# A decoder layer with routed experts: a first token set of seven tiles, routing spread over the attention's steps, marks on GpSimd, later norms on ScalarE

## What is computed

```
x = LN(x + attn(x))        h = LN(x)*gamma + beta; K = h Wk + bk; V = h Wv + bv
                           w = exp((K Wka + bka)/16);  w = w / cumsum(w)
                           attn = cumsum(w * K) * V
x = LN(x + xattn(x, ctx))  softmax(Q K^T / 4, masked) V Wo, 16 heads
logits = x router_w^T + router_b;  top 2 of 8 experts, softmax over the two
x = LN(x + sum over the 2 chosen experts of weight * (gelu(x w1^T + b1) w2^T + b2)) * ln_w + ln_b
```

## Time and profile before

| | us |
|---|---|
| median of 3 runs (542.98 to 546.97) | 543.5 |
| the profiled execution | 543.59 |
| its span on the core | 541.9 |
| TensorE busy | 496.7 (92%) |
| VectorE, ScalarE, GpSimd busy | 374.2, 250.0, 259.8 |

### The profile page before, as it was taken

The page is one execution under the profiler, slowest core; times in us unless marked ns, Lnnn a source line. Parts: engine busy times, 40 slices in busy tenths (PEclk is TensorE's granted clock), DMA queues, the critical chain, the costliest instruction groups (busy, mean ns, idle before and its releaser), DMA issues.

```text
span 541.9 us, 10883 instructions
## 1 busy us (share of the span) xinstructions
PE 496.7 (92%) x3283; PEld 446.7 (82%) x3283; DVE 374.2 (69%) x1111; ACT 250.0 (46%) x835; POOL 259.8 (48%) x370
## 2 busy tenths in 40 slices
PE   6778999989999869988999999999999999999960
PEld 6666888878888757887799999999999999999950
DVE  3777978868768977528877656766676666766644
ACT  3445676656766436652343444433434444333410
POOL 4444132222212320436467656766667666676553
PEclk9999999999999979999999999999999999999995
DMA  8009920836565543426466556666666565666210
GB/s 232 10 7 338 339 86 16 301 110 208 175 222 165 166 132 130 160 58 236 131 205 212 194 197 198 213 222 205 215 209 205 191 221 224 235 221 221 62 49 15
DMA packets 57568, 93.95 MB, mean 173 GB/s; under 512 B 12050, under 2 KB 49305, under 8 KB 52391
## 3 DMA queue, kind: packets, MB, share of 16 engines
q1 hardware_dynamic: 50263, 80.17, 44.2%
q0 software_dynamic: 5616, 12.82, 7.7%
q10 hardware_dynamic: 1632, 0.27, 0.3%
HBM read 65.64 MB, written 30.44 MB: 177 GB/s over the span
## 4 chain that ended last, share of the span: by engine, by line
PE 80%; DVE 11%; issue 3%; POOL 3%; ACT 2%; POOLq 0%; DMA 0%; DVEq 0%; SPq 0%; ACTq 0%
PE psum_a L1690 13%; PE psum_b L1690 12%; PE psum_v L1702 12%; PE psum_c L1702 11%; PE psum_b L1446 8%; PE psum_v L1579 6%; PE psum_a L1545 5%; PE psum_m L1597 2%; PE psum_m L1446 2%; PE psum_c L1566 2%; PE psum_m L1677 1%; PE psum_a L1548 1%; PE psum_c L1561 1%; PE psum_b L1453 1%; DVE front_then_w_ring L1050 1%
## 5 line engine op out<-in xcount | busy, mean ns | idle before, releaser
L954 ACT ACTIVATE front_then_w_ring<-psum_a,front_then_w_ring 128x128 f32<-128x128 f32 x160 | 45.7, 368 | 72.6 <-PE psum_a L1690 71.3
L864 ACT ACTIVATE work<-psum_a,score_max 128x77 f32<-128x77 f32 x256 | 62.2, 334 | 36.2 <-DVE score_max L1121 36.1
L1690 PEld LDWEIGHTS psum_a<-front_then_w_ring 128*128 128x128 f32 x640 | 74.5, 192 | 3.9 <-issue 3.0
L1690 PE MATMUL psum_a<-front_then_w_ring 128*128 128x128 f32 x640 | 75.1, 275 | 2.6 <-ACT front_then_w_ring L944 2.0
L954 ACT ACTIVATE front_then_w_ring<-psum_b,front_then_w_ring 128x128 f32<-128x128 f32 x152 | 43.2, 368 | 69.2 <-PE psum_b L1690 64.5
L1702 PE MATMUL psum_v<-expert_w,front_then_w_ring 128*128 x320 | 72.6, 380 | 0.1
L1690 PEld LDWEIGHTS psum_b<-front_then_w_ring 128*128 128x128 f32 x608 | 70.9, 192 | 0.9
L1690 PE MATMUL psum_b<-front_then_w_ring 128*128 128x128 f32 x608 | 71.1, 275 | 0.0
L1702 PE MATMUL psum_c<-expert_w,front_then_w_ring 128*128 x304 | 68.8, 379 | 0.0
L1702 PEld LDWEIGHTS psum_v<-expert_w,front_then_w_ring 128*128 128x128 f32 x320 | 59.3, 190 | 7.6 <-issue 0.4
L1702 PEld LDWEIGHTS psum_c<-expert_w,front_then_w_ring 128*128 128x128 f32 x304 | 56.3, 190 | 6.9
(11 more groups left out here) (232 smaller groups left out, 891.6 us busy)
## 6 DMA issues: line engine op xcount, KB each, us to landing
front_then_w_ring<-in_w1b SPq DMA_DIRECT2D x39, 1028.0 KB
weighed_outputs<-routing SPq DMA_DIRECT2D x16, 1024.0 KB, 6.7
expert_w<-in_w SPq DMA_DIRECT2D x8, 1024.0 KB, 10.5
weighed_outputs<-work SPq DMA_DIRECT2D x39, 128.0 KB
token_rows<-front_then_w_ring SPq DMA_DIRECT2D x16, 128.0 KB, 2.4
second_buffers<-in_x SPq DMA_DIRECT2D x4, 256.0 KB, 4.6
token_rows<-routing SPq DMA_DIRECT2D x1, 1024.0 KB, 5.3
front_weights_then_tail<-in_b SPq DMA_DIRECT2D x1, 1024.0 KB
```

Source lines behind the costliest of these rows:

```text
L864: last = act.activation(prob[:, u % RING_U, at_k:at_k + SC], pa[:, H % 2, g * SC:(g + 1) * SC], ACT.Exp, bias=smax[:, j % 2, head:head + 1])
L954: last = act.activation(hidT[t % 2][:, c, :], src[:, n, q * P:(q + 1) * P], ACT.Gelu, bias=bias[:, c:c + 1])
L1690: last = pe.matmul(dst[:, n, q * P:(q + 1) * P], w1[:, k, c * P:(c + 1) * P], xtT[t % 2][:, k, :], start=(k == 0), stop=(k == KD - 1))
```

## The change

1. FIRST is 7 instead of 8 and SETS is ((0, 7), (7, 9)): set 0 has 7 tiles and 14 pairs, set 1 has 9 tiles and 18 pairs. 32 more tiles wait for both sets. RANKS_STEP is 50.
2. VectorE's routing of set 0 stands in more steps: three operations at 41 (`first_top`), three at 44 (`first_hot`), the second choice at 47; counts, ranks, and the map's first half at 50, `map_of` and `place_later` at 51, `place` at 52. Marks at 53 to 56.
3. Of each mark pair, GpSimd makes the position one (`mark_slots`), VectorE the column one, with a semaphore of its own.
4. x1's norm from piece 3 on and x2's norm of tiles 0 to 13 are ScalarE's: GpSimd also makes the mean's negative and its product with the root.
5. The first expert tile uses psum_b. Tiles 0 and 1 are turned in steps 61 and 63 (psum_b too), and the passage is written in another order.
6. Second-set marks of GpSimd come in three runs: six pairs behind the row entries, six behind the later map's casts, six behind tile 1's gather (the program's rows below show it). ScalarE's `attention_step` calls `x1_normalise` for pieces from 3 on and `x2_normalise((H - 10) // QUADS)` in the steps that VectorE had. The store column of a tile is no longer limited and the second map column is gone (MAPS 3 to 2).

```diff
-FIRST = 8
+FIRST = 7
...
-SETS = ((0, TILES // 2), (TILES // 2, TILES // 2))
+SETS = ((0, FIRST), (FIRST, TILES - FIRST))
...
-RANKS_STEP = (CHUNKS - 1) * STEPS + 1
+RANKS_STEP = (CHUNKS - 1) * STEPS + 2
...
+                if t >= TILES - 2:
+                    pool.tensor_tensor(x2_rstd[:, j:j + 1], x2_veps[:, j:j + 1], mhalf[:, 0:1], ALU.pow).then_inc(x2_rstd_ready, 1)
+                    return
+                pool.tensor_scalar(x2_drop[:, j:j + 1], x2_mv[:, j, 0:1], -1.0, None, ALU.mult).then_inc(x2_drop_made, 1)
+                pool.tensor_tensor(x2_rstd[:, j:j + 1], x2_veps[:, j:j + 1], mhalf[:, 0:1], ALU.pow).then_inc(x2_pow, 1)
+                pool.wait_ge(x2_drop_made, t + 1)
+                pool.wait_ge(x2_pow, t + 1)
+                pool.tensor_tensor(x2_shift[:, j:j + 1], x2_drop[:, j:j + 1], x2_rstd[:, j:j + 1], ALU.mult).then_inc(x2_rstd_ready, 1)
...
+            def mark_slots(n, first_pair, end):
+                t0, nt = SETS[n]
+                pool.wait_ge(placed, 3 * n + 3)
...
+                for i in range(first_pair, end):
+                    c, t = divmod(i, nt)
+                    pool.tensor_scalar(at_pos[n][:, i], cols, part_n[:, c, t0 + t:t0 + t + 1], None, ALU.is_equal).then_inc(pos_ready, 1)
...
-                if H == RANKS_STEP - 1:
+                if H == RANKS_STEP - 2:
                     weigh(0)
-                if H == RANKS_STEP + 1:
+                if H == RANKS_STEP + 2:
                     map_tiles(0)
                     rows_of_choice(0)
...
+                    mark_slots(0, 0, 4)
+                if H == RANKS_STEP + 4:
+                    mark_slots(0, 4, 9)
+                if H == RANKS_STEP + 5:
+                    mark_slots(0, 9, SET_PAIRS[0])
...
-                if quad == 2 and H >= 10:
-                    x2_normalise((H - 10) // QUADS)
-                if piece_at("x1", H) is not None:
+                if piece_at("x1", H) is not None and piece_at("x1", H) < BY_ACT:
                     x1_normalise(piece_at("x1", H))
...
-                if H == (CHUNKS - 1) * STEPS - 3:
-                    first_choice(0)
-                if H == (CHUNKS - 1) * STEPS - 2:
+                if H == RANKS_STEP - 9:
+                    first_top(0)
+                if H == RANKS_STEP - 6:
+                    first_hot(0)
+                if H == RANKS_STEP - 3:
                     second_choice(0)
                 if H == RANKS_STEP:
                     first_map()
+                if H == RANKS_STEP + 1:
+                    map_of(tbend, spare, FIRST, 0.0)
+                    place_later()
+                if H == RANKS_STEP + 2:
                     place(0)
...
-                where, which = marks_of(n, i)
...
-                dve.tensor_scalar(where, cols, part_n[:, c, t:t + 1], None, ALU.is_equal)
-                dve.tensor_scalar(which, cols, part_n[:, TOPK + c, t:t + 1], token1[:, t:t + 1], ALU.is_equal,
-                                  ALU.mult).then_inc(pos_ready, 1)
+                dve.tensor_scalar(at_col[n][:, i], cols, part_n[:, TOPK + c, t:t + 1], token1[:, t:t + 1], ALU.is_equal,
+                                  ALU.mult).then_inc(col_ready, 1)
...
-            route_logits(TILES - 1)
-            first_choice(LAST)
-            second_choice(LAST)
             indices(2)
             weigh_output(0)
             add_input(0)
+            route_logits(TILES - 1)
+            first_top(LAST)
+            first_hot(LAST)
+            second_choice(LAST)
...
-            for i in range(SET_PAIRS[LAST] // 2):
-                mark(LAST, i)
             dve.wait_ge(ln_in, 2 * 16)
-            indices(3)
             weigh_output(1)
             add_input(1)
             sum_row(0)
-            for i in range(SET_PAIRS[LAST] // 2, SET_PAIRS[LAST]):
+            for i in range(SET_PAIRS[LAST] // 2):
                 mark(LAST, i)
+            row(inner_norm(0))
+            indices(3)
+            sum_row(1)
             later_map()
-            row(inner_norm(0))
-            sum_row(1)
...
                 sum_row(t)
+                if t == 2:
+                    for i in range(SET_PAIRS[LAST] // 2, SET_PAIRS[LAST]):
+                        mark(LAST, i)
...
-                if H == RANKS_STEP + 7:
+                if H == RANKS_STEP + 6:
                     mark_pairs(0)
+                if H == CHUNKS * STEPS - 3:
+                    turn_rows(0)
+                if H == CHUNKS * STEPS - 1:
+                    turn_rows(1)
...
-            for t in range(2, SLOT_TILES):
+            for t in range(3, SLOT_TILES):
+                if t == FIRST - 2:
+                    pe.wait_ge(placed, 3 * LAST + 1)
+                    mark_pairs(LAST)
                 up(t, 0)
                 up(t, 1)
-                if t == 3:
-                    pe.wait_ge(placed, 3 * LAST + 1)
-                    mark_pairs(LAST)
```

236 lines of the change are left out of this document (150 added, 86 removed).

## The result

The changed kernel takes 554.52 us (median of 4 runs, 550.07 to 555.86), the kernel before 543.95 us beside it (4 runs, 542.98 to 546.97). The ratio of the means is 1.017, with a 95% interval of 1.010 to 1.024: slower beyond the noise, by 1 to 2.4%. The prediction said 541.4 us, at most 548, and gave 0.14 to a kernel that is slower by over 1%.

A forecast was written before the change was run, and what follows sets the result against it. TensorE bounds the steady expert tiles at 7.26 us, untouched; the time is decided by how early tile 5 starts. 543.6 − 7.7 (routing) + 5.5 (passage) = 541.4 us, range 531 to 548.

The forecast's parts named there:

- the routing part: First set's routing in the attention steps: −10.0 us from four waits and slow clock, +2.3 new waits, together −7.7 us.
- the passage: From the attention to the experts: late second-set marks start tile 5 3.6 us later, plus 1.9 us clock, +5.5 us.
- All three bounds of the prediction: Upper bounds within the forecast's own case: +4.2 us mark price, +1.7 new waits, +1.1 clock; together rarely at one end.
- The cover of the other new ScalarE norms is the maximum plus the exponentials: Attention steps: 1.4 us of cover against 1.2 us of GpSimd; without it each norm would cost under 1 us.
- … tile 0's and 1's turned rows are made inside the loop … so the 2.04 us go: Passage: turning these rows early, into psum_b, which is free there, removes TensorE's 2.04 us wait.
- The mark's price: One GpSimd mark, a 128x128 compare, m = 0.40 us, bounds 0.29 and 0.76; twelve lie on the passage's chain.
- the slow rival: GpSimd's marks at m = 1 us: +7.2 us on the chain, 550 to 552 us in all; chance 0.12.
- The other terms of the chain: Passage: weights 5.2 us, row entries 1.2, gathers 3.9, row sums 1.3, VectorE's nine marks 2.3; last mark at 277.7.
- The clock behind the idle stretch: After TensorE's idle time ahead of tile 5, slower clock costs 1.9 us, bound below 0, above 3.
- Tile 7's rows … no wait: Rows arrive about 11.4 us behind the marks, wanted 10.8 plus slow clock's loss: no wait, 0.6 us if clock stays up.
- The rule on the shared port: Second set's marks: by the rule VectorE's nine and GpSimd's six alternate, about 2 us more; not added to the sum.
- the forecast's case: Whole kernel as forecast, 537 to 546 us; chance 0.60.

The follow-up runs named there:

- experiment 1: Changed kernel with all of the second set's position marks made by VectorE again, in two runs of nine pairs, none by GpSimd: 545.65 us.
- experiment 3: Token table and tile 7's rows one tile earlier: on experiment 1's kernel 537.83 us; on the changed kernel, marks left as they are, 550.54 us.
- vector_one_run: Changed kernel with VectorE's 18 column marks in one run behind tile 0's row sum, GpSimd's three runs of six kept: 548.98 us.

## Why the prediction failed, point by point

In short: the routing part came out as summed. What failed is the sum for the passage, whose chain was 6.0 us too short (2.4 of it the price of a mark), and three terms that were put at nothing: ScalarE's own norms ahead of the exponentials (2.4 us), the arrival of tile 0's rows (1.5, part of the 6.0) and tile 7's rows (2.7). With the 1.8 us of the start, which is bad luck, this is 12.9 of the 14.5 us between 541.4 and the profiled execution. All three bounds of the prediction at once, 4.2 + 1.7 + 1.1 us, would have given 548.4; most of the miss lay in terms without a bound.

- **The routing part** (−7.7) held: −7.4 between steps 43 and 63. The two new waits stand where they were walked to: 0.47 us at step 50 (0.35) and 1.45 at step 51 (1.9), with the cause foretold, ScalarE's x2 norm waiting for a root behind the first set's weights. (Two of the expectations call them steps 51 and 52.) GpSimd and ScalarE:

```profile
190.11 1.50 POOL L681 TENSOR_TENSOR routing<-routing 128x7 f32<-128x7 f32 x1
...
195.73 0.19 POOL L598 TENSOR_TENSOR routing<-routing 128x1 f32<-128x1 f32 x1
...
195.96 0.60 ACT L957 ACTIVATE front_then_w_ring<-front_then_w_ring,routing 128x256 f32<-128x256 f32 x1 [2.96 <-POOL routing L598]
```

  The reason behind the number was only one of two that would do. I gave the gain to the spreading, with the norms beside it. The runs show that spreading gives the gain between steps 5 and 63 by itself (170.63 us with all norms on VectorE, 170.66 changed), and that with the norms on ScalarE it adds only 1.0 us to what step 50 gives. The wait ahead of the second set's ranks was 1.80 us (2.0).
- **"The cover of the other new ScalarE norms is the maximum plus the exponentials"** failed. That cover is for GpSimd's root. It isn't for ScalarE's own 1.1 us per piece, which stand ahead of the exponentials of the same step, and 2.2 where an input norm stands there too. Price: 2.4 us from step 5 to 43 (120.49 for 118.12), of which 2.0 go when x1's norm moves back (118.54). I had named the bound ("each would cost under 1 us") and left it out of the sum.
- **"… tile 0's and 1's turned rows are made inside the loop … so the 2.04 us go"** left out when the rows arrive. They are now turned in step 61 and were 1.36 us late there, about 1.5 us with the modelled end: they landed 8.6 us after GpSimd's request at 214.37.
- **The mark's price** (m = 0.40) was too low: 0.60 us, still inside the bound of 0.76. Twelve on the chain cost 2.4 us more. The condition of the slow rival, m = 1, was not needed: the kernel became slower at 0.60, since other terms erred the same way.
- **The other terms of the chain** were each short by a little: weights of nine tiles and the row entries +0.7, the first gather to its row sum +0.7, VectorE's nine marks 3.06 us, not 2.3; the casts and gaps 0.7 less. With 1.5 for tile 0's rows, 2.4 for the marks and 0.3 from the last mark to tile 5 this is 5.7 of the 6.0 us by which the passage missed. The other 0.3 is not traced. The mechanism was right: the chain was the one that held tile 5. Its length was not: of some fifteen terms only the casts and gaps came out shorter.
- **The clock behind the idle stretch**: +1.9 forecast, 2.2 measured at tile 5.
- **"Tile 7's rows … no wait"** failed. I put their arrival 11.4 us behind the marks. They were asked for 7.8 us behind the start of tile 5, since the token table stands behind tile 3's row sum and the request behind GpSimd's next root and gather, and took 7.6 us more: 15.4, and 2.21 us of wait with 0.5 around it. (In experiment 1 the same request took 2.9 us; in the changed kernel a w1 load was issued 0.5 us ahead of it, at 287.77.) Seven first tiles, not eight, make tile 7 the first that needs both sets, one tile sooner, but GpSimd asks for it in the same turn of its loop, the fourth, in which it asked for tile 8 before. With the marks mended it cost 7.8 us (experiment 3).
- **The rule on the shared port** would have added 2 us. The Trainium skill's page "SBUF — State Buffer", section "Who interferes with whom", lets VectorE with two SBUF inputs, or in a two-port mode, and GpSimd's reads shut each other out. In vector_one_run GpSimd's six marks took 3.60 us beside VectorE's 18, and 3.50 with VectorE idle; VectorE's took 0.28 each (5.11 us for 18), 0.26 before, with GpSimd idle. The marks don't alternate. Beside VectorE's norms and sums the six took 3.88, 0.4 us more, and VectorE's last nine in the changed kernel, beside GpSimd's bias addition, root and stores, took 0.33 each. So the measurement decides against the 2 us. A mark has one tensor input, so by the rule all hangs on the mode that VectorE runs it in, which no run here shows. The prediction's own row for the rule is weaker than it said: the addition began at 246.49, 0.66 us behind the VectorE operation that it should have held, and both ran at once for 0.19 us. A gather ran beside the operation from 245.51 to 246.46; what stretched it to 0.85 us is not shown.
- **The chances**: the forecast's case held 537 to 546, with the three bounds "together rarely at one end"; that several terms would be short together, and that work moved from VectorE to GpSimd and ScalarE is in order there ahead of something urgent, had too little weight.

## What to carry to other kernels

Work that is moved off a busy engine lands in an in-order queue: price it there by what stands behind it (an exponential, a root, a gather), not by the busy share of the engine. Where a few long instructions have to be made, one run of them beside a chain of round trips is harmless at 0.6 us each; three runs inside that chain held tile 5 by 7.4 us (vector_one_run), and the second engine's half at its end by 3.3 more. When a set of work is made smaller, every request that the next set depends on has to move by as much, and a wait that is taken away uncovers the next one: of some 13 us gained up to and in tile 5, 8.9 arrived until the table was moved too. And parts of a change that cover the same wait are not to be added or ranked from one base: the spreading was worth 1.0 us with the norms on ScalarE and 4.7 with them on VectorE.
